# VectorE's order in the attention loops: the rows' product ahead of the addition of sums, and the block number loaded one step ahead

## What is computed

```python
xl = (x @ Wl + bl).reshape(n, H, C)
xr = (x @ Wr + br).reshape(n, H, C)
e = leaky_relu(xl[src] + xr[dst], 0.2)
logits = einsum('ehc,hc->eh', e, att)
m = segment_max(logits, dst)
p = exp(logits - m[dst])
denom = segment_sum(p, dst)
out = segment_sum(xl[src] * (p / (denom[dst] + 1e-16))[:, :, None], dst).mean(axis=1) + bias
```

## Time and profile before

| what | value |
|---|---|
| time, median of 3 runs (lowest to highest) | 9670.92 us (9669.8 to 9671.51) |
| profiled execution: its time, its span | 9705.39 us, 9703.5 us |
| busy share of VectorE, TensorE (matmuls), GpSimd, ScalarE | 77%, 68%, 52%, 41% |
| mean granted clock of TensorE | 0.758 |
| a group of part A alone (the third layer's first), 48 steps | 150.5 us |
| a group with both parts (the third layer's sixth), of 27, from its first step to the next group's | 185.7 us |
| the first layer's pass with part B alone, 48 steps | 78.0 us |

### The profile page before, as it was taken

One profiled execution on the slowest core, in us unless ns is written; L12 is line 12 of the kernel. 1 busy time (PEld: TensorE's weight loads), 2 busy tenths in 40 slices (PEclk: granted clock), 3 DMA queues, 4 the chain that ended last, 5 costly groups with the idle time before them and its releaser, 6 DMA issues. The chain is left out here.

```text
span 9703.5 us, 180857 instructions
## 1 busy us (share of the span) xinstructions
PE 6644.2 (68%) x27124; PEld 4815.8 (50%) x27125; DVE 7465.0 (77%) x15346; ACT 3973.6 (41%) x14623; POOL 5056.5 (52%) x5548
## 2 busy tenths in 40 slices
PE   1777777775577777775577777776466666666666
PEld 0454555544355555544355545554455555555555
DVE  6677777774577777774577777775699999999999
ACT  0344544451255444452144444443144444444443
POOL 2555555521555555530455555540366666666666
PEclk7898999895799899996689989997555555555555
DMA  2111111110111111110111111110000000000001
GB/s 87 31 31 27 28 28 29 28 14 0 32 29 32 26 28 29 29 20 0 27 28 28 31 27 28 29 26 0 22 17 17 18 17 17 17 17 18 17 17 17
DMA packets 219588, 234.03 MB, mean 24 GB/s; under 512 B 74765, under 2 KB 200718, under 8 KB 219150
## 3 DMA queue, kind: packets, MB, share of 16 engines
q1 hardware_dynamic: 95630, 166.18, 5.9%
q0 software_dynamic: 123776, 66.31, 5.7%
HBM read 219.39 MB, written 12.80 MB: 24 GB/s over the span
## 5 line engine op out<-in xcount | busy, mean ns | idle before, releaser
L490 POOL DMA_INDIRECT xg<-table,idx x2880 | 2916.2, 1013 | 2437.5 <-issue 1341.1
L624 PE MATMUL psum<-px,oh 128*128 128x272 f32 x5760 | 1750.4, 428 | 835.3 <-issue 320.8
L609 PE MATMUL psum<-wz,xt 128*128 x6072 | 1972.4, 419 | 187.6 <-ACT lin L816 94.6
L624 PEld LDWEIGHTS psum<-px,oh 128*128 128x128 f32 x5760 | 1012.2, 196 | 1310.7 <-issue 1020.8
L609 PEld LDWEIGHTS psum<-wz,xt 128*128 128x128 f32 x6072 | 1015.1, 204 | 693.8 <-issue 298.8
L513 POOL DMA_INDIRECT xg<-table,idx x960 | 933.9, 973 | 583.4 <-issue 149.2
L796 ACT ACTIVATE dist<-iota_f,ndloc 128x128 f32<-128x128 f32 x2880 | 998.7, 394 | 464.2 <-PE psum L624 179.7
L1171 DVE TENSOR_TENSOR px<-xs,pg 128x528 f32 (+1 forms) x1440 | 1024.4, 712 | 207.7 <-issue 169.4
L1182 DVE TENSOR_TENSOR acc<-acc,psum 128x272 f32 x1440 | 630.6, 438 | 684.7 <-issue 562.2
L1152 DVE TENSOR_REDUCE lr<-u 128x16 f32<-128x512 f32 x1518 | 1037.6, 686 | 124.6 <-DVE u L1144 83.4
L759 PE MATMUL psum<-acc,oh 128*128 128x32 f32 x1920 | 509.8, 406 | 896.5 <-DVE acc L1508 894.8
(11 more groups left out here) (270 smaller groups left out, 9880.3 us busy)
## 6 DMA issues: line engine op xcount, KB each, us to landing
dr<-dlocs SPq DMA_DIRECT2D x480, 192.0 KB
xg<-table,idx POOLq DMA_INDIRECT x3840
acc<-w_rows SPq DMA_DIRECT2D x160, 192.0 KB
fl<-flags SPq DMA_DIRECT2D x30, 576.2 KB
flags<-fl SPq DMA_DIRECT2D x10, 576.2 KB, 3.2
table<-xn SPq DMA_DIRECT2D x4, 784.0 KB, 3.6
xp<-keys SPq DMA_DIRECT2D x5, 385.0 KB, 4.4
u<-keys SPq DMA_DIRECT2D x5, 385.0 KB, 4.4
```

The costliest lines, as they stand in the source:

```text
L490: nc.gpsimd.indirect_dma_start(out=xg[:, s % S6, t, 96:128], out_offset=None, in_=table, in_offset=bass.IndirectOffsetOnAxis(ap=idx[:, s, ...
L609: pe.matmul(out_z, xt[:, r, e * P:(e + 1) * P], wz[:, bass.ds(l, 1), :].rearrange("p o z -> p (o z)"), start=True, stop=False)
L624: last = pe.matmul(agg_ps(r), oh[:, r, e, :], px[:, r, e, :], start=(e == 0), stop=(e == 1))
```

## The change

Three things in `dve_body`, and nothing on any other engine. The rows' product of step k stands ahead of the addition of step k-2. The load of the block number is taken out of `add_sums` into `block_at`. And where both parts run, the number for the next step's addition is loaded between `weighted` and `over_channels` of this step and kept in a register. The first addition of each body still loads its own number (step 0; in a group's first body step 2, since steps 0 and 1 have no addition there), as do the pass with part B alone and the two additions after each group's last body.

```diff
+            def block_at(k):
+                return v.value_load(brow[0:1, bass.ds(k, 1)], min_val=0, max_val=BLOCKS - 1)
+
-            def add_sums(l, g, k, r):
-                b = v.value_load(brow[0:1, bass.ds(k, 1)], min_val=0, max_val=BLOCKS - 1)
+            def add_sums(l, g, k, r, b):
+
                 v.wait_ge(agg_done, AHEAD + l * NS + k + 1)
                 v.wait_ge(acc_done, AHEAD + l * AGGS + 2 + g + k)
                 sums = acc[:, bass.ds(b, 1), :].rearrange("p o a -> p (o a)")
...
                 for s in range(S6):
                     r = s % 2
-                    if b and (s > 1 or not starts_group):
-                        add_sums(l, g - 1, k0 - GS + s - 2, r)
+                    adds = b and (s > 1 or not starts_group)
                     if b:
                         weigh_rows(l, g - 1, i, k0 - GS + s, s)
+                    if adds and not a:
+                        add_sums(l, g - 1, k0 - GS + s - 2, r, block_at(k0 - GS + s - 2))
+                    if adds and a:
+                        add_sums(l, g - 1, k0 - GS + s - 2, r, block_at(k0 - GS + s - 2) if s == 0 or (starts_group and s == 2) else ahead)
                     if a and s == J:
                         chunk_logits(l, g, i, 0)
...
                     if a:
                         weighted(l, k0 + s, r)
+                    if b and a and s + 1 < S6 and (s > 1 or not starts_group):
+                        ahead = block_at(k0 - GS + s - 1)
+                    if a:
                         over_channels(l, k0 + s, r, (g * BODIES + i) * 2 + s // J, s // J, s % J)
```

More of the change, by code:

```diff
@@ L1209, in dve_group @@
                 if b:
-                    add_sums(l, g - 1, g * GS - 2, 0)
-                    add_sums(l, g - 1, g * GS - 1, 1)
+                    add_sums(l, g - 1, g * GS - 2, 0, block_at(g * GS - 2))
+                    add_sums(l, g - 1, g * GS - 1, 1, block_at(g * GS - 1))
             def early_places(l, g, steps):
```

## The result

The changed kernel took 9591.67 us (median of four runs, 9586.47 to 9601.33) against 9671.22 us of the kernel before on the same chip (9669.8 to 9673.48): a ratio of 0.9919, 95% interval 0.9902 to 0.9936. It is faster by 80 us, where 575 were forecast. In a later comparison the same two kernels took 8878.23 and 9486.9 us: 0.9358 (0.9342 to 0.9373), 609 us. I call the chip of the first comparison the first, those of the next two batches the second and third (kernel before: 9712 and 9717 us), and those of the rest the fourth and fifth (9495 us, and 9487 or 9492 us). The second to the fifth are four different chips; that the first is none of them is taken from the time of the kernel before, as its number is not on record.

The account below looks back on a forecast made before the run. VectorE was taken as the bound, a fifth of its time going to its own sequencer. Six bodies x 3.1 + 1.0 + 1.7 = 21.3 us a group, 27 groups 575 us: 9671 - 575 = 9096 us, range 9000 to 9240, stretched to 9360.

Parts of the forecast that it names:

- What is late next?: Middle bodies after the change: GpSimd needs 17.0 to 17.7 us and binds in part, TensorE needs 14.8 us.
- Per body: Middle bodies: VectorE falls from 20.57 to 17.1 us; 17.45 taken, a gain of 3.1, between 2.5 and 3.45.
- The note on failure in the prediction: Mid-group bodies: the forecast fails if they take over 18.1 us.
- The load hidden: Block number's load behind `u`, ahead of the channel sum: its 0.73 us fit under the wait, costed at nothing.
- rival C: VectorE's load is held until `u` has ended: a step takes 3.26 us, the kernel 9714 us, slower; chance 0.07.
- Rival B: Sequencer was already past the load, something else holds the addition: time within 0.2% of 9671 us; chance 0.05.
- The gain of 0.65 us a step: VectorE's plain step falls from 3.18 to 2.53 us through the new order and the early load.
- The 0.59 us put down to the product's register work: VectorE, between addition and rows' product: register work of 0.59 us, to be hidden under the channel sum.
- VectorE's own 17.1: Middle bodies: VectorE's own time falls by 5 x 0.65 + 0.2 = 3.45 us, to 17.1 us.
- First body and last five steps: Ends of a group: gain 1.0 us (0 to 2.0) in the first body, 1.7 (1.0 to 2.2) in the last.
- Rival A: Gathers, projection and their waits hold bodies with both parts at 19.2 us: time 9415 us; chance 0.18.
- The rule on VectorE's blocking of descriptors: GpSimd can't write gather descriptors under certain VectorE operations; if all six `oht` hit, gain falls to 0.6 us a body.

Follow-up runs that it names:

- four "cures": Changed kernel, fourth chip, against the kernel before: GpSimd product replacing second gather 0.956; half-row gathers 0.934; no loads of places 0.9324; loads of places issued by GpSimd 0.9617.

## Why the prediction was wrong, and where it was right

The step that failed is "What is late next?" in the part "Per body". It named GpSimd, at 17.0 to 17.7 us, and TensorE, at 14.8, and took 17.45. On the first chip what came next was neither; it was the pauses, and the body stayed at 20.60: 238 of 972 steps took 4.92 us, where plain steps of 2.5 to 2.6 were forecast. The sum had no term for them. What makes them stays open. The note on failure in the prediction, bodies over 18.1 us in mid-group, is what came.

*The steps on VectorE* held on all chips. Plain step: 2.53 forecast, 2.48 to 2.60 measured in the steps without a pause and without an addition of logits. The load hidden: yes, and it starts 0.2 us before `u` does, so the instruction queue lets it through; rival C is out, with no channel sum 1.4 us behind `u`'s start. Rival B is out by the same rows. But where the prediction says under B that the trace disagrees with a sequencer that goes on while an operation waits, it says too much: here it does go on. The gain of 0.65 us a step was right, its parts were not. The 0.59 us put down to the product's register work vanish with the early load alone, so nearly all of the gain is the load's.

*Per body, on the fifth chip:* six bodies from 122.1 to 101.0 us in the group above, and over the 27 groups 20.27 to 17.03 us a body, a gain of 3.24 against 3.1. Some luck is in that: both ends of the difference were 0.3 to 0.4 us too high (20.57 and 17.45). VectorE's own 17.1 was a little high: half the gathers gave 16.8 even on the third chip. GpSimd binds at nearly the same point. With two more issues a body in its queue the bodies took 18.3 us, and with part A alone, where half the gathers gave 85.3 us a group (third chip), all of them give (fifth) 125.1 to 125.6, or 16.9 to 17.2 us a body after the first. I had its cycle right at 17.0.

*First body and last five steps:* in that group 1.6 and 2.7 us there, against 1.0 and 1.7 forecast; the means over the 27 groups are 0.7 and 2.4. TensorE's 2.47 us a step did not stop the last steps, which take 2.42 us each in that group.

*Sum:* 22.6 us a group there (156.3 to 133.7 us from the first `u` to the last), times 27 is 610 us; measured 609, forecast 575. So the 575 us were a good sum where there are no pauses. On the first chip 80 came.

*Rival A* had the right warning for the wrong reason. I took part A's 150.5 us a group for what gathers and projection need together. On the fifth chip that group takes 125.6 us in the kernel before, so the other 25 us belong to where it ran and not to the work. What they are is known in part only. None of the 102 slow operations lies in a group of part A alone. Stretches of over 0.4 us in which no engine works add up to 6.4 us a group there, and to none on the fifth chip; the rest is not accounted for. The low clock, 0.75 against 0.97, does not explain them: in these three groups the steps after the first body that began at half clock took 2.64 us in the mean, those at full clock 3.65. As a number rival A was nearer (9415 us against 9592), but still 177 us off: with the denser step there were over five times as many slow operations.

*The rule on VectorE's blocking of descriptors.* In the kernel before, the middle bodies have 255 gathers of over 1.2 us among 1933, and an `oht` starts under every one of them; their mean is 1.43 us. (Under 520 gathers that stayed short one starts too, so it is not enough by itself.) So the prediction read that row rightly, and the rule that it took from the Trainium skill ("SBUF — State Buffer", the "DVE blocks DMA" trap), that GpSimd can't write a gather's descriptors under certain VectorE operations, agrees with the trace in kind. A denser step did not make more hits: on the fifth chip the long gathers were 237 of 1933 before and 228 of 1845 after, and on the first 255 and then 90 of 1926, where the pauses moved the gathers about. The 0.7 us a body that I had added for them comes to 0.6 on the fifth chip (12 x the mean of 1.002 less the median of 0.953).

*What the row could have told.* The idle of 16.0 us before additions was VectorE's, and its removal is seen. But the bodies of before, at a granted clock of 1.00, could not tell how often pauses would come with a denser step. The maximum of 737 ns beside a median of 305 on the line that I was costing was there to be asked for, and the low clock of part A alone was left as an argument instead of being explained.

## What to carry to other kernels

Read the maximum beside the median of the sequencer's small operations (loads of a register, checks, semaphore waits). If a 23 ns check sometimes takes 0.7 us while no engine works, something outside the kernel's own operations takes time, and a gain worked out from busy and idle times can be taken back whole. When the kernel before itself differs by 2% between two batches, compare variants only with the changed kernel in the same batch; four "cures" here cured nothing. For a register loaded by an engine with waits of its own, put the load behind the last operation that still waits in the queue: that alone gave 0.7 us a plain step, the reordering beside it nothing more. (The two halves by themselves ran only where there were pauses, so what each is worth in the whole time without them is not shown.)

## What the runs showed of the hardware

- Two levels for one kernel: 9671 to 9717 us on the first three chips, 9487 to 9495 us on the other two, and for the changed kernel 9592 against 8878.
- VectorE's sequencer loads a register while an operation issued before still waits in the queue (load at 1412.2, `u` at 1412.44).
- GpSimd's elementwise work slows VectorE's. In the run (fourth chip) with a product of 0.83 us on GpSimd a step, the six bodies' rows (group by line: busy, mean ns, idle before) are

```profile
L499 POOL TENSOR_TENSOR spare<-xn 128x280 f32<-128x280 f32 x36 | 29.9, 831 | 0.7
L1179 DVE TENSOR_TENSOR px<-xs,pg 128x528 f32 (+1 forms) x36 | 29.3, 813 | 1.9 <-ACT xs L816 1.9
...
L1147 DVE TENSOR_SCALAR oht<-dr,iota_p 128x256 bf16<-128x256 bf16 x37 | 18.3, 494 | 0.2
```

  where `oht` took 291 ns and the product 702 with gathers alone (fifth chip): bodies of 18.4 us instead of 17.0.
- With part A alone GpSimd's pace is 16.9 to 17.1 us for twelve gathers and two copies, whether a row has 64 or 128 bytes (fifth chip); in the whole time half rows gained 0.2%.
- A gather under which an `oht` starts can take longer: in the middle bodies of the kernel before 255 of 775 such gathers took over 1.2 us (1.43 in the mean, the median of all is 0.955), and no gather without one did.
